# A graph attention layer on one core: two more steps gather x alone, the first multiplication inside the pairs' chain, flag lines by ScalarE, and another release for the gathers

## The reference

```python
hl = x @ Wl.T + bl
hr = x @ Wr.T + br
s = (jnp.take(hl, src, axis=0) + jnp.take(hr, dst, axis=0)) * alpha
s = jnp.where(s >= 0, s, SLOPE * s)
smax = jax.ops.segment_max(s, dst, num_segments=n_nodes)
e = jnp.exp(s - jnp.take(smax, dst, axis=0))
denom = jax.ops.segment_sum(e, dst, num_segments=n_nodes)
att = e / jnp.take(denom, dst, axis=0)
msg = jnp.take(x, src, axis=0) * att
return _layernorm(x + jax.ops.segment_sum(msg, dst, num_segments=n_nodes))
```

## Time and profile before

| | |
|---|---|
| median of three runs | 1437.57 us (1435.41 to 1439.32) |
| span of the profiled execution | 1129.4 us |
| own time of the profiled execution | not shown; the three times lie 306 to 310 us above the span |
| busy: TensorE / VectorE / ScalarE / GpSimd | 1079.0 / 1072.6 / 998.6 / 820.7 us |
| DMA | 212 MB, 188 GB/s on average |

### The profile page before, as it was taken

The page is one execution under the profiler, slowest core; times in us unless marked ns, Lnnn a source line. Parts: engine busy times, 40 slices in busy tenths (PEclk is TensorE's granted clock), DMA queues, the critical chain, the costliest instruction groups (busy, mean ns, idle before and its releaser), DMA issues.

```text
span 1129.4 us, 34988 instructions
## 1 busy us (share of the span) xinstructions
PE 1079.0 (96%) x9403; PEld 1014.7 (90%) x9403; DVE 1072.6 (95%) x1526; ACT 998.6 (88%) x2606; POOL 820.7 (73%) x858
## 2 busy tenths in 40 slices
PE   6879999999999999999999999999999999999984
PEld 5779999999999999999999999999999899999863
DVE  7889999999999999999999999999999999999967
ACT  4359999999999999999999999999999889998996
POOL 5577777777777777777777777777777777777770
PEclk9889999999999999999999999999999999999997
DMA  9887776666667776767766666677676666676533
GB/s 227 290 221 191 192 187 191 190 188 188 191 187 191 189 189 187 192 189 190 189 189 188 189 191 190 188 189 188 191 189 185 186 188 182 187 191 183 143 99 114
DMA packets 231064, 211.97 MB, mean 188 GB/s; under 512 B 46375, under 2 KB 204286, under 8 KB 230788
## 3 DMA queue, kind: packets, MB, share of 16 engines
q0 software_dynamic: 39872, 108.39, 35.5%
q1 hardware_dynamic: 190442, 100.03, 32.4%
q10 hardware_dynamic: 565, 1.33, 0.4%
HBM read 198.95 MB, written 11.47 MB: 186 GB/s over the span
## 4 chain that ended last, share of the span: by engine, by line
PE 51%; POOL 26%; issue 11%; ACT 3%; DVE 2%; DMA 0%; ACTq 0%; POOLq 0%; DVEq 0%
POOL xg L435 25%; PE ps_w L654 19%; PE ps_sT L590 11%; PE ps_u L630 9%; PE ps_z L608 5%; PE ps_q L599 2%; PE ps_u L636 2%; PE ps_qT L618 2%; ACT attr L853 1%; DVE stats L1161 1%; ACT acc L802 0%; DMA xg<-gather_rows,srcT 0%; ACT right L811 0%; DVE acc L1086 0%; ACT ex L749 0%
## 5 line engine op out<-in xcount | busy, mean ns | idle before, releaser
L435 POOL DMA_INDIRECT xg<-gather_rows,srcT x808 | 764.9, 947 | 253.0 <-issue 235.9
L654 PE MATMUL ps_w<-onehot,ex 128*128 128x128 f32 x3328 | 405.7, 275 | 1.2 <-ACT acc L806 1.2
L654 PEld LDWEIGHTS ps_w<-onehot,ex 128*128 128x128 f32 x3328 | 388.4, 192 | 1.8 <-issue 1.6
L1095 DVE TENSOR_TENSOR_SCAN ps_F<-line,B,ps_sT 128x512 f32<-128x512 bf16 x208 | 266.1, 1279 | 1.0 <-issue 1.0
L1100 DVE TENSOR_TENSOR_SCAN B<-line,ps_F 128x512 f32<-128x512 bf16 x208 | 254.0, 1221 | 7.2
L630 PEld LDWEIGHTS ps_u<-right,onehotT 128*128 128x128 f32 x1664 | 208.5, 192 | 18.9 <-issue 0.2
L630 PE MATMUL ps_u<-right,onehotT 128*128 x1664 | 221.1, 276 | 0.0
L802 ACT ACTIVATE acc<-ps_w 128x768 f32 x208 | 168.7, 811 | 23.5
L1105 DVE TENSOR_TENSOR z<-ps_sT,B 128x512 f32<-128x512 f32 x208 | 143.9, 692 | 7.1
L1121 DVE TENSOR_TENSOR ex<-ps_z,xg 128x512 f32<-128x512 f32 x208 | 141.7, 681 | 5.7 <-ACT ps_z L773 5.7
L1129 DVE TENSOR_TENSOR v<-ps_u,attr 128x512 f32<-128x512 f32 x208 | 141.8, 682 | 0.3
(11 more groups left out here) (264 smaller groups left out, 1164.1 us busy)
## 6 DMA issues: line engine op xcount, KB each, us to landing
attr<-edge_attr_in SPq DMA_DIRECT2D x832, 64.0 KB
line<-step_lines SPq DMA_DIRECT2D x182, 128.0 KB
xg<-gather_rows,srcT POOLq DMA_INDIRECT x808
gather_rows<-acc SPq DMA_DIRECT2D x12, 512.0 KB, 6.0
line<-soon_lines SPq DMA_DIRECT2D x26, 128.0 KB
edge<-step_lines SPq DMA_DIRECT2D x182, 4.0 KB
acc<-x_in SPq DMA_DIRECT2D x6, 448.0 KB, 7.6
xg<-x_in SPq DMA_DIRECT2D x6, 448.0 KB, 5.6
```

The source lines that it names most:

```text
L435: pool.indirect_dma_start(out=xg[:, k % SLOTS, i, :], out_offset=None, in_=rows_dram, in_offset=bass.IndirectOffsetOnAxis(ap=srcT[:, k * W ...
L654: last = nc.tensor.matmul(columns, ex[:, (k - 1) % 2, c, i, :], onehot[:, (k - 1) % 3, i, :], start=(i == 0), stop=(i == WIDE - 1), skip_g ...
L1095: V.tensor_tensor_scan(ps_F[:, :], line[:, k % LINES, 0:GE], ps_sT[:, :], B[:, (k - 1) % 3, GE - 1:GE], ALU.add, ALU.max).then_inc(F_ok, 1)
```

## The change

The diff does four things. AHEAD goes from 6 to 8, so that steps 6 and 7 gather x alone too; their gathers need the pairs' tables to be used up (srcf_ok, step_ok), the transposes get two more places in PSUM, and each waits for the copy of the one before it but one. VectorE's bodies -2 and -1 (h and v of steps 0 and 1) move from behind the preparation into it: -2 ahead of rel2, -1 behind sq, for which sq moves from v to ex. The flag lines (row 0) are made by ScalarE from diff, which gets its own signal, and ScalarE's waits for the pairs' tables come one body later. And a row gather waits for v of step k - lead + 1 in place of the transposes of z of step k - lead.

```diff
-    AHEAD = 6
+    AHEAD = 8
...
-        sq = v[0:PR, :, :, :].rearrange("p a i d -> p a (i d)")
+        sq = flat(ex[:, 1, :, :, :])[0:PR, :].rearrange("p (a d) -> p a d", a=2)
...
+                if k == 7:
+                    pool.wait_ge(srcf_ok, 2)
+                    pool.wait_ge(step_ok, 1)
                 for i in range(WIDE):
                     pool.indirect_dma_start(
                         out=xg[:, k, i, 0:D], out_offset=None, in_=x,
...
             for k in range(AHEAD, STEPS):
-                if k == 7:
-                    pool.wait_ge(srcf_ok, 2)
-                    pool.wait_ge(rel_ok, 1)
+                if k == AHEAD:
                     pool.wait_ge(ahead_ps, 3)
-                if k == 8:
                     pool.wait_ge(u_ps, 2)
...
                 if k >= lead:
-                    pool.wait_ge(z_ps, k - lead + 1)
+                    pool.wait_ge(v_ok, k - lead + 2)
...
-                if k == 5:
-                    pe.wait_ge(ahead_sb, 4)
+                if k >= 5:
+                    pe.wait_ge(ahead_sb, k - 1)
...
                 if k == 0:
-                    ahead(5)
+                    for a in range(5, AHEAD):
+                        ahead(a)
...
                 body(k)
-                if k == -4:
+                if k == -3:
                     act.wait_ge(rel_ok, 1)
+                    nc.scalar.activation(lines[:, :, 0, :], halves(diff), ACT.Copy, scale=-BIG).then_inc(high_ok, 1)
+                    act.wait_ge(rel_ok, 2)
                     nc.scalar.activation(lines[:, :, 1, :], halves(rel2), ACT.Copy, scale=-2.0).then_inc(high_ok, 1)
                     act.wait_ge(sq_ok, 1)
                     nc.scalar.activation(lines[:, :, 2, :], sq, ACT.Copy).then_inc(high_ok, 1)
-                if k == -3:
-                    act.wait_ge(lines_ok, 4)
+                if k == -2:
+                    act.wait_ge(lines_ok, 3)
+                    act.wait_ge(high_ok, 3)
```

On VectorE (the functions of the steps now stand ahead of the preparation, unchanged) the end of the preparation reads:

```diff
+            V.tensor_scalar(diff[:, :, 0], row(12), -1.0, 1.0, ALU.mult, ALU.add).then_inc(rel_ok, 1)
+            body(-2)
+            chained(V.tensor_tensor(rel2, dst_f, first128[:, :, None].broadcast_to([PR, 8, P]), ALU.subtract))
+
+            V.tensor_scalar(rel2, rel2, -1.0, float(P), ALU.max, ALU.min).then_inc(rel_ok, 1)
+            dve.wait_ge(rel_ok, 2)
+            V.tensor_tensor(sq, halves(rel2), halves(rel2), ALU.mult).then_inc(sq_ok, 1)
+            body(-1)
...
+            dve.wait_ge(high_ok, 3)
+            V.tensor_tensor(lines[:, :, 3, :], sq, lines[:, :, 2, :], ALU.subtract).then_inc(lines_ok, 1)
...
+            for k in range(STEPS + 1):
                 body(k)
```

More of the change, by code:

```diff
@@ L193, in build_gnn_layer @@
         ps_heads, ps_D = ps_w[:, 0, 0:3 * PR], ps_w[0:PR, 1, 0:P + 2]
-        ps_ahead = [ps_qT[:, :], ps_w[:, 1, :], ps_qT[:, :], ps_w[:, 0, :], ps_w[:, 1, :], ps_w[:, 0, :]]
+        ps_ahead = [ps_qT[:, :], ps_w[:, 1, :], ps_qT[:, :], ps_w[:, 0, :], ps_w[:, 1, :], ps_w[:, 0, :],
+                    ps_w[:, 1, :], ps_w[:, 0, :]]
         ps_t = [ps_z, ps_F]
@@ L905, in block_of, with ratio @@
                 chained(V.tensor_copy(dest, i_tile[0:parts, 1, :]))
+            u_of = lambda bank: bank[:, :].rearrange("p (i d) -> p i d", i=WIDE)
+            def ratio(c):
+                cols = slice(c * CH * P, (c + 1) * CH * P)
+                if c < SHARED:
+                    dve.wait_ge(near_ok, 2 * c + 2)
+                else:
+                    dve.wait_ge(recip_ok, c + 1)
+                    V.tensor_tensor(acc[:, 0, cols], acc[:, 0, cols], recip[:, cols], ALU.mult)
+                    chained(V.tensor_tensor(acc[:, 1, cols], acc[:, 1, cols], recip[:, cols], ALU.mult))
+                V.scalar_tensor_tensor(out=acc[:, 1, cols], in0=acc[:, 0, cols], scalar=-2.0, in1=acc[:, 1, cols],
+                                       op0=ALU.add, op1=ALU.mult).then_inc(ratio_ok, 1)
@@ new lines, in body @@
+            def body(k):
+                if has(k):
+                    dve.wait_ge(line_in[k % LINES], 16 * (k // LINES + 1))
+                    dve.wait_ge(sT_ps, k + 1)
+                    if k >= 1:
+                        dve.wait_ge(B_ok, k)
+                    V.tensor_tensor_scan(ps_F[:, :], line[:, k % LINES, 0:GE], ps_sT[:, :],
+                                         B[:, (k - 1) % 3, GE - 1:GE], ALU.add, ALU.max).then_inc(F_ok, 1)
+                    dve.wait_ge(F_ok, k + 1)
+                    if k >= 2:
+                        dve.wait_ge(gap_ok, k - 1)
+                    V.tensor_tensor_scan(B[:, k % 3, ::-1], line[:, k % LINES, GE:0:-1], ps_F[:, ::-1], -BIG,
+                                         ALU.add, ALU.max).then_inc(B_ok, 1)
+                    dve.wait_ge(B_ok, k + 1)
+                    if k >= 2:
+                        dve.wait_ge(z_ps, k - 1)
+                    V.tensor_tensor(z[:, k % 2, :], ps_sT[:, :], B[:, k % 3, :], ALU.subtract).then_inc(z_ok, 1)
+                if has(k + 2):
+                    j = (k + 2) % SLOTS
+                    dve.wait_ge(rows_in[j], 16 * (WIDE - 1) * ((k + 2) // SLOTS + 1))
+                    dve.wait_ge(u_ps, k + 3)
+                    if k + 2 < AHEAD:
+                        V.tensor_tensor(u_of(ps_u), u_of(ps_u), both[:, :, :].broadcast_to([P, WIDE, D]), ALU.add).then_inc(h_ok, 1)
+                    else:
+                        V.tensor_tensor(u_of(ps_u)[:, 1:WIDE, :], u_of(ps_u)[:, 1:WIDE, :], xg[:, j, 1:WIDE, D:ROW], ALU.add)\
+                            .then_inc(h_ok, 1)
+                if k == STEPS:
+                    ratio(0)
+                if has(k - 1):
+                    dve.wait_ge(e2_ok, k)
+                    if k >= 3:
+                        dve.wait_ge(sums_ps, k - 2)
+                    V.tensor_tensor(ex[:, (k - 1) % 2, 1, :, :], u_of(ps_z),
+                                    xg[:, (k - 1) % SLOTS, :, 0:D], ALU.mult).then_inc(msg_ok, 1)
+                if has(k + 2):
+                    j = (k + 2) % ATTRS
+                    dve.wait_ge(attr_in[j], 64 * ((k + 2) // ATTRS + 1))
+                    dve.wait_ge(h_ok, k + 3)
+                    if k >= 0:
+                        dve.wait_ge(sT_ps, k + 1)
+                    V.tensor_tensor(v[:, k % 2, :, :], u_of(ps_u), attr[:, j, :, :], ALU.mult).then_inc(v_ok, 1)
+                if k == STEPS:
+                    for c in range(1, EARLY):
+                        ratio(c)
@@ L1054, in _ @@
             V.tensor_tensor(diff[:, :, 1:P], dst_f[:, :, 1:P], dst_f[:, :, 0:P - 1], ALU.not_equal)
-            V.tensor_scalar(diff[:, :, 0], row(12), -1.0, 1.0, ALU.mult, ALU.add)
+            V.tensor_scalar(diff[:, :, 0], row(12), -1.0, 1.0, ALU.mult, ALU.add).then_inc(rel_ok, 1)
+            body(-2)
             chained(V.tensor_tensor(rel2, dst_f, first128[:, :, None].broadcast_to([PR, 8, P]), ALU.subtract))
             V.tensor_scalar(rel2, rel2, -1.0, float(P), ALU.max, ALU.min).then_inc(rel_ok, 1)
-            dve.wait_ge(rel_ok, 1)
+            dve.wait_ge(rel_ok, 2)
             V.tensor_tensor(sq, halves(rel2), halves(rel2), ALU.mult).then_inc(sq_ok, 1)
-            V.tensor_scalar(lines[:, :, 0, :], halves(diff), -BIG, None, ALU.mult).then_inc(lines_ok, 1)
+            body(-1)
             def sources(h):
@@ L1067, in _ @@
             sources(0)
-            dve.wait_ge(high_ok, 2)
+            dve.wait_ge(high_ok, 3)
             V.tensor_tensor(lines[:, :, 3, :], sq, lines[:, :, 2, :], ALU.subtract).then_inc(lines_ok, 1)
@@ L1134, in _ @@
-            u_of = lambda bank: bank[:, :].rearrange("p (i d) -> p i d", i=WIDE)
-            for k in range(-2, STEPS + 1):
+            for k in range(STEPS + 1):
                 body(k)
```

54 lines of the change are left out of this document (removed).

## The result

| kernel | median, us (runs) | span of the profiled run | clock |
|---|---|---|---|
| before | 1438.44 (1435.41 to 1439.35, 4) | 1129.4 shown ahead, 1436.9 in a later run | 0.981 (later run) |
| after | 1814.09 (1810.65 to 1816.99, 4) | 1810.7 | 0.835 |

The ratio is **1.263 [1.260, 1.266]**: the change makes the kernel 26% slower, where 1432.6 us was forecast.

A forecast was written before the change was run, and what follows sets the result against it. GpSimd's gather stream, 5.00 us a step against VectorE's 4.84, was taken as the bound. Slots 1.72 us late but 4.56 earlier, plus the stream's 2.5 us in hand, start step 16 5.0 us sooner: 1437.6 to 1432.6 us, range 1429.9 to 1436.4.

The forecast's parts named there:

- The sum's frame: Whole run: span falls from 1129.4 to 1124.4 us, some 308 us around it stay untouched, so 1437.6 becomes 1432.6.
- Part 5: Row gathers' wait, moved to v: old one costs nothing now, 1.6 us in the new kernel; new one never binds.
- GpSimd waiting after step 16: Sign of error: from step 16 on the gather stream was to go at 5.00 us a step and stay last.
- Part 1: Steps 6 and 7 fill GpSimd's 7.09 us of standing early on: 7.8 us at most, limited by when slots free.
- F(0): VectorE's first scan (line 1095) of step 0, forecast at 62.11 us instead of 66.67.
- Part 2: First multiplication put inside the chain of the pairs' tables: VectorE's idle 3.80 us goes, with 0.09 of overlap.
- Parts 2 and 3: VectorE's front: 3.80 us idle and 0.09 overlap go, flag lines on ScalarE save 0.67; step 0's first scan 4.56 earlier.
- Part 4: Work that steps 6 and 7 add on TensorE and ScalarE: step 6's first scan comes 1.72 us late.
- step 16 at 103.03 us: Start of step 16's gathers on GpSimd, at 103.03 instead of 108.07 us: the gain of 5.0 us.
- (b): Rival: steps 6 and 7's gathers locked out beside VectorE's densest stretch; gain 3.5 us, 1434.1 us; chance 0.12.
- (d): Rival, slower: the flag lines' store lands late, ScalarE stands at step 1, every slot comes later; 1442.5 us; chance 0.06.

The follow-up runs named there:

- r1: The kernel before, unchanged, run and profiled again on chip A: 1439.19 us, ratio 0.999, span 1436.9 us.
- r3: The kernel before with only the row gathers' wait changed, to v instead of z's transposes, on chip A: 1813.46 us, ratio 1.259.
- r2: The kernel after with the old wait on z's transposes put back, on chip A: 1443.87 us, ratio 1.002 against the kernel before.
- r14: The kernel after with the old wait and six steps instead of eight gathering x alone, on chip D: 1131.56 us, ratio 1.000 against before.
- r9: The kernel before with all gathers kept, each reading rows of half the length from step 10 on, on chip C: 1416.58 us, ratio 1.001.
- r13: The kernel before with two of each step's four gathers replaced by four GpSimd multiplications from step 10 on, on chip D: 1123.04 us, ratio 0.992.
- r17: The kernel before with two of each step's four gathers replaced by four GpSimd multiplications, run once more on chip D: 1122.84 us, ratio 0.993.
- r4: The kernel before with one more GpSimd wait, once, ahead of step 12's gathers, on z's transposes of step 7, chip B: 1430.99 us, ratio 1.012.
- r8: The kernel before with two of each step's four gathers left out from step 10 on, on chip C: 1137.01 us, ratio 0.805.
- r6: The kernel before with the gathers' lead wait moved to u_ps, a TensorE count shortly before v, on chip B: 1470.83 us, ratio 1.040.

## Why the prediction was wrong

- **The sum's frame.** It took 308 us as lying around the span, "and nothing in the change touches them". That is the step that failed first. They are steps of 6.30 us in place of 4.84; where they are there is no free stream of gathers, and the whole sum is of another regime. It was to be seen that something was missing: 21% of the time had no row.
- **Part 5, the release.** "Never binds", since GpSimd's pace of 5.00 us was slower than the consumer's 4.84. Where gathers hold TensorE up, the consumer is slower than GpSimd and the lead wait stops GpSimd before nearly every step: 334.5 us in r1, 690.3 in after. And its kind decides, TensorE's count or VectorE's, which no step of the prediction weighed: 372.5 us (r3 against before). The prediction had named GpSimd waiting after step 16 as a sign that it was wrong, and so it was.
- **Part 1, eight steps.** On chip A the eight x gathers in a row lie over TensorE's last matmuls for gather_rows. VectorE's last addition to them and F(0), in r1 and then in r2 (between them h(1), the addition whose idle time Part 2 is about):

```profile
57.51 0.28 DVE L916 TENSOR_TENSOR acc<-ps_sT,both 128x128 f32<-128x128 f32 x1
...
78.72 0.70 DVE L1111 TENSOR_TENSOR ps_u<-ps_u,both 128x512 f32<-128x512 f32 x1 [3.94 <-PE ps_u L630]
...
80.14 1.28 DVE L1095 TENSOR_TENSOR_SCAN ps_F<-line,B,ps_sT 128x512 f32<-128x512 bf16 x1
```

```profile
65.84 0.29 DVE L981 TENSOR_TENSOR acc<-ps_sT,both 128x128 f32<-128x128 f32 x1 [5.05 <-remote]
...
80.51 0.70 DVE L949 TENSOR_TENSOR ps_u<-ps_u,both 128x512 f32<-128x512 f32 x1 [0.55 <-PE ps_u L631]
...
84.09 1.29 DVE L933 TENSOR_TENSOR_SCAN ps_F<-line,B,ps_sT 128x512 f32<-128x512 bf16 x1
```

  TensorE's matmuls for the addition end at 59.12 in r2, but the addition waits until 1.8 us after the run of gathers (54.34 to 64.04 us) is over, 8.33 us later than in r1. F(0) is 3.95 us later, most of the 4.7 by which r2 is behind r1: a cost where the sum had a gain. On chip D this part wasn't tried with eight steps.
- **Parts 2 and 3, the front.** The mechanism was right in both regimes. Forecast were 4.56 us and F(0) at 62.11; r14 has 62.25. In r2 VectorE's idle time for u(1) is 0.55 us where r1 has 3.94; its last addition is 8.33 us late and F(0) only 3.95, so 4.38 us are made good. It was also right that an early F(0) is worth nothing while the stream starts no earlier.
- **Part 4**, the 1.72 us, and step 16 at 103.03 us: open. They need the eight steps on a chip like D.
- **The rivals.** None had it. (b), GpSimd locked out by VectorE, looked at the right engine from the wrong side: a row gather takes 946 to 949 ns on average in every kernel but r9 (943, half rows), r13 and r17 (977); it is they that hold others up. The Trainium skill, "SBUF — State Buffer" (Who interferes with whom), names the ports that VectorE and GpSimd share as the only place of contention; read as the full list, it would let no gather cost TensorE anything, and r4's stretch, 65 matmuls against 216, decides against that reading. The slower side, (d), took a late store for its price, and no wait of the change.

**What stays open.** How a run of gathers reaches TensorE. Late in a run its matmuls start some 0.7 us or multiples of it apart, and its counts arrive some 1 to 2 us after the run has ended. Whether SyncE is hit too isn't told: four loads of attr take it 4.06 us to issue at 395.92 in after and 1.91 outside a run, but in the profile shown ahead, beside an unbroken stream of gathers, the same four take anything from 1.91 to 3.29 us (between 400 and 440 us). VectorE's and ScalarE's instructions keep their lengths. That TensorE lives for the first 5 us of a run on what it has in hand, and that this is why eight gathers hold the scan up 7.1 us where four cost 1.46, is argued from the timelines, not shown. How much of the 26% is TensorE's lower clock wasn't split off either: in after its 3328 matmuls into ps_w take 518.9 us, in r1 425.9. Nor is it known what sets chip D apart.

## What to carry to other kernels

A profile whose span is a fifth short of the measured time may well be of an execution unlike the timed ones: run the unchanged kernel once and look before you add up a gain. On four of these five chips a long unbroken run of gathers by GpSimd stalls TensorE, so ask of any wait on GpSimd's queue not only when it lets go but how many gathers it lets go at once; here a wait on TensorE's own count kept the runs at four and was worth 26%. And an idle stretch of GpSimd that looks free to fill may be what lets TensorE finish.

## What the runs showed of the hardware

- A run of GpSimd's gathers slows TensorE on four of five chips: 24 us of it leave 65 matmuls of 216 (r4). On these chips TensorE's counts come late beside gathers even where its matmuls keep their pace: 1.46 us (median) for ps_sT in r1, 0.01 in the profile shown ahead and in r14 (chip D), 0.01 in r8 with half the gathers. The bytes don't matter (1.001 [0.998, 1.004] with half of them), the number does (0.805 with half).
- Its cost isn't linear in the length of a run: four gathers (4.7 us) cost a step 1.46 us, eight (9.7 us) hold VectorE's scan up 7.1 us, twenty (24.7 us) hold its next two waits up 11.08 and 10.23 us.
- On such chips the kernel with a wait of GpSimd on a count of VectorE takes 21 to 26% longer than with the old wait on TensorE's; with another of TensorE's counts 4% longer (r6), most of it where VectorE's count is still the last.
- The granted clock falls along with TensorE's idle time: 0.98 in r1, 0.85 and less in after. From 396 to 424 us r1 has the full clock (1.00) and its steps take 6.3 us all the same, so there the clock isn't the cause.
- One kernel, on five chips: 1131, 1413, 1414, 1415, and on chip A 1441 us first and 1412 later.
